# Transposes ahead of the scores, values behind V's copy, norms in pairs, and new orders on ScalarE and VectorE, in a gated state-space and local-attention block

## The reference

```python
x = x + attn(shift_tokens(x))      # per layer, 6 layers
x = x + ffn(shift_tokens(x))
# attn: 16 heads of 64, windows of 32 that see themselves and the window before
qkv = x @ Wqkv
q, k = l2norm(q) * q_scale, l2norm(k) * k_scale     # then rotary with xpos scales
sim = einsum(q, k) * 8, masked outside the last 32 keys
out = softmax(sim) @ v, then @ Wo
```

## Time and profile before

| | |
|---|---|
| Runs, median of 3 | 2237.3 us (2233.07 to 2239.87) |
| The profiled execution's own time | 2229.49 us |
| its span, first to last instruction | 2227.6 us |
| mean granted TensorE clock | 0.977 |
| busy share PE, DVE, ACT, POOL | 93%, 73%, 66%, 56% |
| first mask matmul of step 0 | at 371.9 us |

### The profile page before, as it was taken

The page is one execution under the profiler, slowest core; times in us unless marked ns, Lnnn a source line. Parts: engine busy times, 40 slices in busy tenths (PEclk is TensorE's granted clock), DMA queues, the critical chain, the costliest instruction groups (busy, mean ns, idle before and its releaser), DMA issues. The chain is left out here.

```text
span 2227.6 us, 82947 instructions
## 1 busy us (share of the span) xinstructions
PE 2062.4 (93%) x32996; PEld 1476.9 (66%) x32996; DVE 1627.3 (73%) x3071; ACT 1472.3 (66%) x4549; POOL 1238.2 (56%) x1377
## 2 busy tenths in 40 slices
PE   7788888999899999999998999999999989999997
PEld 3232335985776976876867859768768678587672
DVE  1598986985876966867857759668678577596673
ACT  4532326976775967867767759668678667596682
POOL 1465865764753754854647537548546465365450
PEclk9888989999999999999999999999999999999999
DMA  1321202111121211211111212112211111121010
GB/s 59 133 72 60 75 29 79 41 40 33 42 74 30 50 36 33 65 56 37 40 34 37 79 27 50 35 36 55 64 37 42 34 35 42 28 50 28 24 31 19
DMA packets 148094, 104.31 MB, mean 47 GB/s; under 512 B 15778, under 2 KB 140256, under 8 KB 146176
## 3 DMA queue, kind: packets, MB, share of 16 engines
q1 hardware_dynamic: 147712, 99.07, 16.0%
HBM read 48.31 MB, written 1.18 MB: 22 GB/s over the span
## 5 line engine op out<-in xcount | busy, mean ns | idle before, releaser
L1133 ACT ACTIVATE PR<-ps,MN 128x64 f32<-128x64 f32 x1536 | 356.6, 315 | 391.3 <-DVE MN L1255 391.1
L1383 POOL TENSOR_TENSOR QK<-PC,PS 128x256 f32<-128x256 f32 x384 | 278.9, 726 | 601.0 <-DVE PS L1294 584.1
L1388 POOL TENSOR_TENSOR QK<-QK,RN 128x512 f32<-128x512 f32 x384 | 401.6, 1046 | 158.0 <-ACT RN L1123 130.5
L1002 PE MATMUL ps<-W,XS 128*128 128x256 f32 x1536 | 396.5, 381 | 4.6 <-PEq L64 4.1
L973 PE MATMUL ps<-V,PT 64*32 64x65 f32 x12288 | 301.0, 219 | 1.2
L1002 PEld LDWEIGHTS ps<-W,XS 128*128 128x128 f32 x1536 | 262.7, 191 | 25.6 <-issue 4.9
L1384 POOL TENSOR_TENSOR QK<-PC,PS 128x256 f32<-128x256 f32 x384 | 279.1, 727 | 0.0
L988 PE MATMUL ps<-ident,QK 128*128 128x128 f32 x1536 | 252.0, 287 | 29.3 <-POOL QK L1388 29.3
L973 PEld LDWEIGHTS ps<-V,PT 64*32 64x32 f32 x12288 | 257.6, 105 | 11.3 <-ACT PT L1174 5.9
L1255 DVE TENSOR_REDUCE MN<-ps 128x4 f32<-128x256 f32 x384 | 161.6, 421 | 141.7 <-PE ps L953 135.7
L1278 DVE TENSOR_REDUCE SS<-SQ 128x8 f32<-128x512 f32 x384 | 259.3, 675 | 4.4 <-ACT SQ L1165 4.4
(11 more groups left out here) (138 smaller groups left out, 3439.5 us busy)
## 6 DMA issues: line engine op xcount, KB each, us to landing
V<-V SPq DMA_DIRECT2D x384, 97.5 KB, 2.3
scr<-B_rows SPq DMA_DIRECT2D x32, 512.0 KB, 3.5
V<-V SPq DMA_DIRECT2D x288, 32.5 KB, 2.2
W<-in_Wqkv SPq DMA_DIRECT2D x40, 192.0 KB, 2.8
TC<-in_tcos SPq DMA_DIRECT2D x6, 1024.0 KB, 5.3
TS<-in_tsin SPq DMA_DIRECT2D x6, 1024.0 KB, 8.5
WO<-in_Wo SPq DMA_DIRECT2D x6, 512.0 KB, 4.3
W<-in_W SPq DMA_DIRECT2D x6, 341.0 KB, 3.5
```

The source lines that it names most:

```text
L1002: mm = nc.tensor.matmul(ps[:, par, k * 2 * P:(k + 1) * 2 * P], cols[k], W[:, i, 0:2, :].rearrange("p t m -> p (t m)"), start=True, stop=True)
L1133: e = nc.scalar.activation(PR[:, m % 2, h, slot * DH:(slot + 1) * DH], ps[:, 4 + h, slot * DH:(slot + 1) * DH], ACT.Exp, scale=-1.0, bias= ...
L1383: nc.gpsimd.tensor_tensor(QK[:, par, :, 0:hd], PC[:, par, :, 0:hd], PS[:, par, :, hd:DH], ALU.add)
L1388: nc.gpsimd.tensor_tensor(QK[:, par, :, :], QK[:, par, :, :], bcast_last(RN[:, par, :], DH), ALU.mult).then_inc(qk, 1)
```

## The change

- PE: q and k are transposed ahead of the scores, one iteration later than before (m = n - 4), and ahead of them out_transposed now waits in every iteration for exponents and copy_out of the iteration before. The scores wait for the copy of q and k of their own step. Scores and values go through eight tile positions (row group, column quad) in an order that alternates between row groups; values of the two slots go to banks 5 and 6, a bank for each row group. Values wait for the shifted V, for normalise and for copy_v. The v projection goes to the second half of bank 5 and waits for normalise of this iteration; P's transposes go to the second half of bank 6. Out transposes and scores use banks 3 and 4.
- ACT: a new order, copy_qk, norm_pair, exponents, squares, copy_out, copy_p, copy_v. The logarithm and the root of two steps are one instruction each, of 16 columns, in odd iterations (norm_pair). copy_out writes the columns in another order.
- DVE: least, normalise, tables, norms, clamp_pair. norms works on the iteration's own step (m = n) with no clamp; clamp_pair clamps two steps at once in even iterations, against a constant in place of a tile LEAST. normalise reads two banks.
- POOL: rotate one iteration later (m = n - 2), with the pair's roots; the memset of LEAST goes.

```diff
-SS = sb("SS", [P, 2, 8])
-RN = sb("RN", [P, 2, 8])
+SS = sb("SS", [P, 2, 16])
+RN = sb("RN", [P, 2, 16])
...
-def slot_quad(j):
-    return (j % 4) // 2, (j // 4) * 2 + j % 2
+def window(slot, quad):
+    return quad // 2 * 4 + slot * 2 + quad % 2
+
+spread_tiles = [(0, 0), (1, 2), (0, 1), (1, 3), (0, 2), (1, 0), (0, 3), (1, 1)]
...
-        if n >= NSTEPS:
-            wait(pe, pr, min(n - 5, NSTEPS))
-            wait(pe, oT, m)
+        wait(pe, pr, min(n - 5, NSTEPS))
+        wait(pe, oT, m)
         pe.wait_ge(on, m + 1)
         for k in range(2):
             src = ON[:, m % 2, :, :].rearrange("p (k h) d -> p k (h d)", k=2)[:, k, :]
-            mm = nc.tensor.transpose(ps[:, 4, (1 + k) * P:(2 + k) * P], src, ident[:])
+            mm = nc.tensor.transpose(ps[:, 3, (1 + k) * P:(2 + k) * P], src, ident[:])
         mm.then_inc(oT_ps, 1)
...
     def scores(n):
...
         b, l, i, s, par = place(m)
         if m == 0:
             pe.wait_ge(s_ones, 2)
-        if n >= NSTEPS:
-            wait(pe, pr, m)
-            wait(pe, oT, m - 3)
+        wait(pe, pr, m)
+        wait(pe, oT, m - 3)
         for h in range(2):
-            if h == 0:
-                wait(pe, qkT, min(n - 3, NSTEPS))
-            if h == 1 and n >= 7:
-                pe.wait_ge(v_sh[(n - 7) % 4], 32 * ((n - 7) // 4 + 1))
-            nc.tensor.matmul(ps[:, 4 + h, 0:P], identb[:], MASKB[:, int(s == 0), h, :], start=True, stop=True)
-        for h in range(2):
-            for j in range(8):
-                slot, quad = slot_quad(j)
-                c0 = PAD + s * STEP + j * WIN
-                mm = nc.tensor.matmul(ps[32 * quad:32 * quad + 32, 4 + h, slot * DH:(slot + 1) * DH],
+            nc.tensor.matmul(ps[:, 3 + h, 0:P], identb[:], MASKB[:, int(s == 0), h, :], start=True, stop=True)
+        pe.wait_ge(qkT, m + 1)
+        for slot in range(2):
+            for h, quad in spread_tiles:
+                c0 = PAD + s * STEP + window(slot, quad) * WIN
+                mm = nc.tensor.matmul(ps[32 * quad:32 * quad + 32, 3 + h, slot * DH:(slot + 1) * DH],
                                       QKT[DH * h:DH * h + DH, 0, c0:c0 + WIN],
                                       QKT[DH * h:DH * h + DH, 1, c0 - WIN:c0 + WIN],
                                       start=False, stop=True, skip_group_check=True)
...
         pe.wait_ge(pT, m + 1)
-        if n >= NSTEPS + 5:
-            pe.wait_ge(v_sh[m % 4], 32 * (m // 4 + 1))
-            wait(pe, on, m)
+        pe.wait_ge(v_sh[m % 4], 32 * (m // 4 + 1))
+        wait(pe, on, m)
+        wait(pe, v_cp, min(n, NSTEPS))
         for h in range(2):
-            for j in (0, 2, 1, 3, 4, 6, 5, 7):
-                slot, quad = slot_quad(j)
+            for slot, quad in spread_tiles:
+                j = window(slot, quad)
                 r = slice(64 * slot, 64 * slot + 64)
-                q = j % 4
-                g = (j // 4) * 2 + h
-                mm = nc.tensor.matmul(ps[32 * q:32 * q + 32, 6, g * (DH + 1):(g + 1) * (DH + 1)],
+                mm = nc.tensor.matmul(ps[32 * quad:32 * quad + 32, 5 + slot, h * (DH + 1):(h + 1) * (DH + 1)],
                                       PT[r, m % 2, h, 32 * quad:32 * quad + 32],
                                       V[r, 2 * (m % 8) + j // 4, 2 * (1 - j % 2) + h, :], start=True, stop=True)
         mm.then_inc(o_ps, 1)

     def qk_transposed(n):
-        m = n - 3
+        m = n - 4
         if not 0 <= m < NSTEPS:
             return
+        wait(pe, qkT, m)
         pe.wait_ge(qk, m + 1)
-        if n < 5:
-            wait(pe, qkT, m)
...
         wait(pe, v_cp, n)
+        wait(pe, on, n - 6)
         for k in range(2):
-            if k == 1:
-                wait(pe, pr, n - 4)
-            mm = nc.tensor.matmul(ps[:, 3, k * P:(k + 1) * P], cols[k], W[:, i, 2, :], start=True, stop=True)
+            mm = nc.tensor.matmul(ps[:, 5, (2 + k) * P:(3 + k) * P], cols[k], W[:, i, 2, :], start=True, stop=True)
         mm.then_inc(v_ps, 1)

     def p_transposed(n):
         m = n - 6
         if not 0 <= m < NSTEPS:
             return
-        if n >= NSTEPS:
-            pe.wait_ge(pr, m + 1)
-            wait(pe, v_cp, NSTEPS)
-        if n < 8:
-            wait(pe, pT, m)
+        wait(pe, pT, m)
+        wait(pe, on, m)
+        pe.wait_ge(pr, m + 1)
         for h in range(2):
-            if h == 1 and n < NSTEPS:
-                wait(pe, oT, n - 7)
-            mm = nc.tensor.transpose(ps[:, 3, (2 + h) * P:(3 + h) * P], PR[:, m % 2, h, :], ident[:])
+            mm = nc.tensor.transpose(ps[:, 6, (2 + h) * P:(3 + h) * P], PR[:, m % 2, h, :], ident[:])
         mm.then_inc(pT_ps, 1)
...
         out_transposed(n)
+        qk_transposed(n)
         scores(n)
         values(n)
-        qk_transposed(n)
...
-    def root(n):
-        m = n - 2
-        if not 0 <= m < NSTEPS:
-            return
-        act.wait_ge(lns, m + 1)
-        wait(act, qk, m - 1)
-        nc.scalar.activation(RN[:, m % 2, :], SS[:, m % 2, :], ACT.Exp, scale=-0.5, bias=lnb[:]).then_inc(rn, 1)
+    def norm_pair(n):
+        p = (n - 3) // 2
+        if n % 2 == 0 or not 0 <= p < NSTEPS // 2:
+            return
+        act.wait_ge(ssm, p + 1)
+        nc.scalar.activation(SS[:, p % 2, :], SS[:, p % 2, :], ACT.Ln, scale=LN_SCALE).then_inc(lns, 1)
+        act.wait_ge(lns, p + 1)
+        wait(act, qk, 2 * p - 2)
+        nc.scalar.activation(RN[:, p % 2, :], SS[:, p % 2, :], ACT.Exp, scale=-0.5, bias=lnb[:]).then_inc(rn, 1)
...
-        nc.scalar.copy(OT[:, s // 2, i, (s % 2) * STEP:(s % 2 + 1) * STEP], ps[:, 4, P:3 * P]).then_inc(oT, 1)
+        nc.scalar.copy(OT[:, s // 2, i, (s % 2) * STEP:(s % 2 + 1) * STEP].rearrange("p (w k c) -> p k w c", w=2, k=2),
+                       ps[:, 3, P:3 * P].rearrange("p (k w c) -> p k w c", k=2, w=2)).then_inc(oT, 1)
...
-        root(n)
+        copy_qk(n)
+        norm_pair(n)
         exponents(n)
+        if u == U_FFN and t >= 0:
+            load_set(nc, act, GELU)
+        squares(n)
         copy_out(n)
-        if u == U_FFN and t >= 0:
-            logs(n)
-            load_set(nc, act, GELU)
-        copy_qk(n)
-        squares(n)
         copy_p(n)
         copy_v(n)
         if u == U_FFN and t >= 0:
             gates(t, n)
             load_set(nc, act, EXP_LN)
-        else:
-            logs(n)
...
-        o = ps[:, 6, 0:4 * (DH + 1)].rearrange("p (a d) -> p a d", d=DH + 1)
+        o = ps[:, 5:7, 0:2 * (DH + 1)].rearrange("p s (h d) -> p s h d", h=2)
+        inv = RC[:, m % 2, :].rearrange("p (s h) -> p s h", s=2)
         wait(dve, on, m - 1)
-        nc.vector.reciprocal(RC[:, m % 2, :].unsqueeze(2), o[:, :, DH:DH + 1]).then_inc(rc, 1)
+        nc.vector.reciprocal(inv.unsqueeze(3), o[:, :, :, DH:DH + 1]).then_inc(rc, 1)
         dve.wait_ge(rc, m + 1)
         wait(dve, oT_ps, m - 1)
-        nc.vector.tensor_tensor(ON[:, m % 2, :, :], o[:, :, 0:DH], bcast_last(RC[:, m % 2, :], DH),
-                                ALU.mult).then_inc(on, 1)
+        nc.vector.tensor_tensor(ON[:, m % 2, :, :].rearrange("p (s h) d -> p s h d", s=2), o[:, :, :, 0:DH],
+                                bcast_last(inv, DH), ALU.mult).then_inc(on, 1)
...
     def norms(n):
-        m = n - 1
-        if not 0 <= m < NSTEPS:
-            return
-        dve.wait_ge(sq, m + 1)
-        wait(dve, rn, m - 1)
-        nc.vector.tensor_reduce(SS[:, m % 2, :], SQ[:, m % 2, :, :], AX.X, ALU.add).then_inc(ss, 1)
-        dve.wait_ge(ss, m + 1)
-        nc.vector.tensor_tensor(SS[:, m % 2, :], SS[:, m % 2, :], LEAST[:], ALU.max).then_inc(ssm, 1)
+        if n >= NSTEPS:
+            return
+        p, k = n // 2, n % 2
+        dve.wait_ge(sq, n + 1)
+        wait(dve, rn, p - 1)
+        nc.vector.tensor_reduce(SS[:, p % 2, 8 * k:8 * k + 8], SQ[:, n % 2, :, :], AX.X, ALU.add).then_inc(ss, 1)
+
+    def clamp_pair(n):
+        p = n // 2 - 1
+        if n % 2 or not 0 <= p < NSTEPS // 2:
+            return
+        dve.wait_ge(ss, 2 * p + 2)
+        nc.vector.tensor_scalar(SS[:, p % 2, :], SS[:, p % 2, :], 1e-24, None, ALU.max).then_inc(ssm, 1)
...
         normalise(n)
+        tables(n)
         norms(n)
-        tables(n)
+        clamp_pair(n)
...
     def rotate(n):
-        m = n - 1
+        m = n - 2
...
-        pool.wait_ge(rn, m + 1)
-        nc.gpsimd.tensor_tensor(QK[:, par, :, :], QK[:, par, :, :], bcast_last(RN[:, par, :], DH),
+        pool.wait_ge(rn, m // 2 + 1)
+        nc.gpsimd.tensor_tensor(QK[:, par, :, :], QK[:, par, :, :], bcast_last(RN[:, m // 2 % 2, 8 * par:8 * par + 8], DH),
```

More of the change, by code:

```diff
@@ L780, in transformer_block @@
         lnb = sb("lnb", [P, 1])
-        LEAST = sb("LEAST", [P, 8])
         QKT = sb("QKT", [P, 2, PAD + L])
@@ L815, in transformer_block @@
         stored = [sem("stored%d" % c) for c in range(NCH)]
-        s_vz, s_ones, s_v0, s_lnb, s_least = (
-            sem(k) for k in ("s_vz", "s_ones", "s_v0", "s_lnb", "s_least"))
+        s_vz, s_ones, s_v0, s_lnb = (
```

(18 more changed lines are left out.)

1 line of the change is left out of this document (removed).

## The result

The changed kernel takes 2318.46 us (median of 4, 2314.46 to 2319.40) against 2235.72 us before (median of 4): ratio 1.0365, 95% interval 1.0343 to 1.0386. It is slower by 83 us; the forecast was 2333 us, with a range of 2290 to 2390. The profiled executions took 2314.46 and 2229.49 us, so 85 us are to be found in the traces.

What follows compares the result with a forecast made beforehand. PE bounds plain steps at 3.47 us; after the change its wait for copy_out makes them 3.80. +93 - 4 + 7 = +96 us on 2229.5 gives 2325, plus 7.8 for the median: 2333 us, range 2290 to 2390.

Steps and rivals of the forecast that it cites:

- The ring: Plain steps: PE's next out transposes wait for copy_out behind exponents and squares; 3.80 us a step against 3.47; chance 0.79.
- the second branch: Path into squares through scores, values and q/k projection, then copy_out: 3.75 us with values at 0.43, 4.00 at 0.68.
- the first: Path into squares through scores, minimum and exponents, then copy_out: summed to 3.77 us, taken as 3.80.
- squares released by the projection: Sign of being wrong: squares released by the q/k projection rather than by exponents, the 4.00 us branch.
- The count: Of 384 steps, 283 are plain; 283 x (3.80 - 3.47) = +93 us.
- The steps with extra work: Seven or eight steps per phase, extra work covering PE's wait: -0.05 x 77 = -4 us, bounds -19 to +8.
- Behind the second variance: ACT, busy with the inverse, starts exponents at 2.6 in place of 1.98, uncovered: 0.6 x 11 = +7 us.
- Norms in pairs at zero: Paired norms relieve ACT and DVE, but neither ends the wait for copy_out: zero gain.
- stay at POOL's pace: The four steps with rotary table scaling, where POOL is fullest, keep 19.55 us for four: zero change.
- the rival: DVE's clamp collides with POOL's product, 0.5 us more every second step: +71 on top, 2403 us; chance 0.10.
- The faster rival: Earlier minimum, squares and copy leave PE's own 3.2 to 3.4 us as the step: 2214 or 2141 us; chance 0.06.
- the halved scores: Spread tiles halve the scores' flight; halved issue of 0.33 us gives 0.17 us, not the 0.3 needed.

Runs made afterwards that it cites:

- experiment 2: The changed kernel with one more 128 x 1 copy on ACT between exponents and squares in every step: 2321.85 us, ratio 1.0401.
- experiment 3: The changed kernel with the first of the two q/k projection matmuls run twice in every step: 2452.73 us.
- experiment 8: The changed kernel with the scores in the old order, all of one head and then all of the other: 2333.80 us.
- experiment 11: The kernel before, with the feed-forward step's logarithm moved behind the gates and the table reload: 2227.96 us against 2234.53, ratio 0.9969.
- experiment 10: The changed kernel, copy_out still late, with norms unpaired (logarithm, root and clamp in every step): 2300.27 us, ratio 1.0306 to the kernel before.
- experiment 9: The changed kernel with copy_out ahead of squares, norms unpaired and seven implied waits on PE left out: 2184.73 us, ratio 0.9792.
- experiment 1: The changed kernel with copy_out moved ahead of squares on ACT: 2200.95 us, ratio 0.9855 to the kernel before.
- experiment 4: The changed kernel with the values' 16 products quad by quad, both row groups of a quad together, same banks: 2317.65 us.
- experiment 7: The changed kernel with copy_out ahead of squares and without seven waits on PE that other waits imply: 2186.77 us, ratio 0.9791.

## Why the prediction was right

The forecast was +96 us; measured are +83 by the medians and +85 between the profiled executions. PE waits for the late copy_out in plain steps, as forecast, and that is the bulk of the time.

**The ring.** Forecast 3.80 us, measured 3.81. Term by term in the timeline above: OT's end to L930 0.10 (0.10), L930 to the scores 0.89 (0.86), scores to minimum 0.58 (0.67), minimum to exponents 0.46 (0.45), exponents to squares 0.92 (0.81), squares to OT 0.49, OT 0.37 (0.39). 0.09 us came off the scores and 0.11 went onto the exponents, because squares waited for the projection there. That is the second branch, at 0.10 + 0.89 + 0.33 + 0.46 + 1.17 + 0.49 + 0.37 = 3.81 (forecast 3.75). I had put the first at 3.77, taken as 3.80, and let it bind; experiments 2 and 3 say that the second binds, and experiment 8 agrees. So the meeting of 3.80 and 3.81 is partly luck: the branch that binds was summed 0.06 us too short, and the one that I took, with 0.81 from exponents to squares, would have come to 3.70. In the list of what would show the forecast wrong I had put squares released by the projection, together with a step of 4.00. The release was so; the step was not, since values took 0.46 us, near the 0.43 taken and not 0.68.

**The count.** 283 x (3.82 - 3.47) = 99 us against +93, 3.82 being the mean of the plain steps away from a phase's extra work. PE's recorded gaps ahead of L930 add up to 93.7 us, the same size, though not the same quantity, since PE's own work fell as well.

**The steps with extra work.** Forecast -4, measured about -21, which is the largest error of a term. The six steps with out-projection, mean and variance became shorter by 0.03 to 0.26 us each, 0.9 in a phase, -10 us. I read this as the 0.2 us of values arriving there, with the v projection's new wait taking less of it than I had allowed; no run separates the two. The feed-forward step became shorter by 0.94, -11 us, to which I had given nothing: I had priced what ACT does in a step but not what of it lies ahead of the table load that the gates wait for (experiment 11).

**Behind the second variance.** Forecast +7. The first step behind is 4.18, +0.37 over the plain one, and the next 4.04, +0.23: 11 x 0.6 = +6.6. The size came out right with help from luck: the busy ACT that I had priced at 0.6 is at most the other two thirds, and a third is the pair's root by experiment 10, which I had not seen.

**Norms in pairs at zero** was wrong: they cost 13 to 21 us in the changed kernel. I had looked at whether a pair's root is in time for PE in plain steps, where it is, and wrote that the table steps "stay at POOL's pace". They stayed at 19.6 us for four, but not for that reason: with single norms they take 16.2. The longer step would have given POOL the time it lacked, and the pairs took it. Against the kernel before, this error does not show in the sum, because the time stayed where it had been.

Sum: +99 - 10 - 11 + 7 = +85 us, the 85 between the profiled executions. The terms are rounded means, so an agreement to the last 2 or 3 us is chance.

**The rivals.** In the changed kernel the clamp did not collide in plain steps; its median is 165 ns and its longest 633 over 192 clamps:

```profile
L1263 DVE TENSOR_SCALAR SS<-SS x192: 160/165/633, 366.6 to 2237.8; 128x16 f32<-128x16 f32 x192
```

The 22 above 300 ns, one at the start and the others in feed-forward and table steps, agree with the rule of the Trainium skill (page "SBUF — State Buffer", section "Who interferes with whom") that such an instruction and GpSimd can block one another: one of 0.63 us stands at 1033.10, behind the start of POOL's addition (L1367, 1032.96), and ends with it at 1033.7. In plain steps POOL stands still at that time, as forecast. But the rival is real: with a clamp in every step and copy_out first it does collide, 0.72 us against 0.16 (experiment 9). The faster rival lives in experiment 1: with the ring below PE's own work the usual step is 3.30 us, inside its 3.2 to 3.4. It was not the halved scores that opened it, since scores to minimum fell only from 0.67 to 0.58, but the place of copy_out.

## What to carry to other kernels

In a pipeline written out by hand, add up for each engine the ring that returns to its first instruction of the next step, every time an order is changed: here PE, DVE and ACT all had room, and with one copy behind squares instead of ahead of them the usual step was 3.81 us instead of 3.30. A release that another engine waits for goes ahead of work that only its own engine needs. Putting two steps' small instructions into one means that the first step waits for the second; count that wait in the steps in which the consumer is already late, not in the plain ones. And look at the length of even the smallest DVE instruction from step to step: where it changes from 0.16 to 0.72 us, see whether it ends with an instruction of POOL.

## What the runs showed of the hardware

PE's first weight load stood 0.07 us behind the end of the ACT copy that released it. An fp32 matmul of 256 columns costs 0.43 us at the full clock, twice what one of its records suggests (experiment 3). Sixteen 64x32 products with 65 columns to either of two banks took 0.46 us from their start to the full-size matmul behind them, 0.68 with one bank and half of the tile positions; their order made no difference (experiment 4), while that of the scores ahead of them made 0.07 us (experiment 8). Seven waits that hold nothing up cost a PE that is the bound 0.02 us in the usual plain step, 0.05 in the mean, and 14 us over the kernel (experiment 7). A 128x8 clamp of SBUF against a constant took 0.16 us alone and 0.72 beside a POOL addition that had begun 0.04 us earlier; all 147 clamps above 0.3 us in that trace end with a POOL instruction (experiment 9). A 128x1 copy on ACT that was busy for 0.21 us let the next instruction begin after 0.08 (experiment 2).
